# Tying GpSimd's row scatter to TensorE's gate products in an attention and mixture-of-experts kernel

## What is computed

```python
def ffn(x):                                   # 8192 tokens x 256
    scores = softmax(x @ gate_w.T)            # 8 experts
    idx = top_k(scores + gate_b, 2)           # each token goes to 2 of the 8
    cw = sum(one_hot(idx) * scores_at(idx))
    a = swiglu((x @ w1[e] + b1[e]) * (x @ w3[e] + b3[e]))   # every expert e, width 512
    routed = sum over e of cw[:, e] * (a @ w2[e] + b2[e])
    shared = swiglu((x @ sw1 + sb1) * (x @ sw3 + sb3)) @ sw2 + sb2
    return routed + shared
```

## Time and profile before

| | us |
|---|---|
| median of 3 executions | 2370.92 |
| the three | 2356.42, 2370.92, 2376.85 |
| the profiled execution | 2381.0 |
| its span, first to last instruction | 2379.3 |

### The profile page before, as it was taken

The page is one execution under the profiler, slowest core; times in us unless marked ns, Lnnn a source line. Parts: engine busy times, 40 slices in busy tenths (PEclk is TensorE's granted clock), DMA queues, the critical chain, the costliest instruction groups (busy, mean ns, idle before and its releaser), DMA issues. The chain is left out here.

```text
span 2379.3 us, 38346 instructions
## 1 busy us (share of the span) xinstructions
PE 2135.5 (90%) x14197; PEld 1310.5 (55%) x14197; DVE 1558.3 (65%) x2267; ACT 1720.2 (72%) x2176; POOL 687.6 (29%) x694
## 2 busy tenths in 40 slices
PE   5995999999999999999996956789999999999970
PEld 4773333333333333333335855568788888888860
DVE  4663255555555555555556965456788888888878
ACT  4664999999999999999994743223466666666645
POOL 1111000000000000000002525556056666666644
PEclk9997999999999999999998967789999999999995
DMA  5886744555555544444405845656477777777666
GB/s 186 301 301 176 130 90 89 100 99 100 100 97 99 88 72 91 85 87 62 74 10 163 285 146 200 198 182 208 165 218 195 173 169 171 171 171 172 173 171 233
DMA packets 174588, 356.88 MB, mean 150 GB/s; under 512 B 18440, under 2 KB 101000, under 8 KB 167112
## 3 DMA queue, kind: packets, MB, share of 16 engines
q1 hardware_dynamic: 140140, 299.86, 47.2%
q0 software_dynamic: 31952, 46.82, 11.0%
q10 hardware_dynamic: 2316, 7.80, 0.9%
HBM read 210.85 MB, written 143.42 MB: 149 GB/s over the span
## 5 line engine op out<-in xcount | busy, mean ns | idle before, releaser
L1076 ACT ACTIVATE att_prob<-att_scores 128x1024 f32<-128x1024 f32 (+2 forms) x1122 | 997.6, 1035 | 58.6 <-PE att_scores L1022 56.1
L1041 PE MATMUL att_out<-att_prob,att_va 128*32 128x512 f32 (+3 forms) x5000 | 576.7, 542 | 12.9 <-DVE att_prob L1108 12.9
L1022 PE MATMUL att_scores<-att_qs,att_ks 50*128 50x512 f32 (+3 forms) x2560 | 465.9, 430 | 20.7 <-DMA att_qs<-guard 16.7
L1022 PEld LDWEIGHTS att_scores<-att_qs,att_ks 50*128 50x128 f32 x2560 | 211.1, 185 | 492.5 <-ACT att_prob L1076 418.2
L1690 POOL DMA_INDIRECT sums<-moe_y,moe_token x156 | 348.7, 2235 | 235.3 <-ACT moe_y L1941 189.2
L1828 PE MATMUL moe_ps<-moe_xt_hi,moe_w_hi 128*128 128x512 f32 x880 | 352.9, 401 | 11.0 <-ACT moe_h L1914 9.4
L1828 PE MATMUL moe_ps<-moe_xt_lo,moe_w_hi 128*128 128x512 f32 x880 | 348.8, 396 | 5.6 <-issue 5.6
L1828 PE MATMUL moe_ps<-moe_xt_hi,moe_w_lo 128*128 128x512 f32 x880 | 350.3, 398 | 3.6 <-issue 3.6
L970 POOL DMA_DIRECT2D ctx_scr<-att_cout x64 | 55.5, 867 | 983.1 <-DVE att_cout L1158 944.2
L1108 DVE SCALAR_TENSOR_TENSOR att_prob<-att_prob,att_tri 128x512 f32<-128x512 f32 x224 | 144.8, 688 | 268.5 <-ACT att_prob L1076 268.5
L1914 ACT ACTIVATE moe_h<-moe_ps,moe_wb 128x512 f32<-128x512 f32 x220 | 148.4, 676 | 168.9 <-PE moe_ps L1828 100.5
(11 more groups left out here) (232 smaller groups left out, 3216.1 us busy)
## 6 DMA issues: line engine op xcount, KB each, us to landing
qk_parts<-proj_qk SPq DMA_DIRECT2D x64, 512.0 KB
keep_first_weights<-w_experts SPq DMA_DIRECT2D x22, 1412.0 KB
moe_wraw<-w_experts SPq DMA_DIRECT2D x21, 1412.0 KB
att_qs<-qk_parts SPq DMA_DIRECT2D x180, 128.0 KB
att_ks<-qk_parts SPq DMA_DIRECT2D x180, 128.0 KB
rows_in<-att_zeros SPq DMA_DIRECT2D x13, 1548.0 KB, 21.5
moe_moved<-tokens SPq DMA_DIRECT2D x32, 512.0 KB
keep_first_rows<-rows_in SPq DMA_DIRECT2D x20, 516.0 KB
```

The source lines that it names most:

```text
L1022: last = nc.tensor.matmul(pss[e % SBUFS][:, h, at:at + CH - q0], ks[s][rows, half, kt * P:(kt + 1) * P], qs[s][rows, half, c * CH + q0:(c ...
L1041: last = nc.tensor.matmul(pso[k % 2][strip, q0:], va[team % 2][:, kt, strip], probs_of(u)[:, h, at:at + CH - q0], start=(kt == 0), stop=(i ...
L1076: nc.scalar.activation(probs_of(u)[:, half * 2:half * 2 + 2, start:], pss[e % SBUFS][:, :, start:], ACT.Exp, scale=HD ** -0.5)\
```

## The change

Ahead of every scatter GpSimd now also waits for a count of gate products. For scatter q the count is `(q - 8) * 13 * 4 // 128`, rounded down; where it is zero or less there is no wait. It is 1 for q = 11, 12 for q = 38 and 39, 13 for q = 40, and 48 for q = 127, which is the last gate product of step 11. The count is turned into a step and a block, and the wait is on that step's `p1` semaphore. Nothing is removed and nothing else moves: the same 128 scatters, in the same order, from the same buffers.

```diff
+        SCATTERS = 2 * TPC * NCH
+        LEAD = 2 * TPC
+
+        def follow_products(pool, q):
+
+            blocks = (q - LEAD) * (FIRST - 1) * FB // SCATTERS
+            if blocks > 0:
+                c, f = divmod(blocks - 1, FB)
+                pool.wait_ge(p1[c % 2], c // 2 * FB + f + 1)
+
         with nc.Block() as block:
             @block.gpsimd
             def _(pool):
@@
                     for r in range(2):
                         for j in range(TPC):
                             t = c * TPC + j
+                            follow_products(pool, (c * 2 + r) * TPC + j)
                             pool.indirect_dma_start(
                                 out=rows_in, out_offset=bass.IndirectOffsetOnAxis(slot[:, r, t:t + 1], 0),
                                 in_=moved[s][:, r, j, :], in_offset=None).then_inc(scattered[s], 16)
```

## The result

The changed kernel took 2343.76 us (median of 7, 2342.20 to 2348.66) against 2371.42 for the kernel before (7 executions, 2356.42 to 2376.85). The ratio is 0.9885 with a 95% interval of 0.9863 to 0.9908: 27.7 us less, 1.15%. I had forecast 12 us less, with a range that held the time. The direction and the place were right and the size was too small by more than half: two terms of the sum, what the first stall would still cost and what would follow it, were each too small by nearly 8 us. The experiments then showed something larger: the stalls that the change shortens are there in some sessions on the chip and absent in others, for the same kernel, and where they are absent the change is worth nothing. In the traces the recording itself differs between the two kinds of session, so whether the gain exists when nothing is recorded is open.

A forecast was written before the change was run, and what follows sets the result against it. It took TensorE as the bound, with 48.2 us lost in three stalls during scattering. Lost after: 18.3 + 12 + 5.8 = 36.1, a gain of 12.1 from 2370.92, so 2359 us; 8-in-10 range 2332 to 2382.

The forecast's parts named there:

- A: Stall at 1483 to 1517 us, in steps 1 and 2: 27.9 us lost before, 18.3 forecast to remain.
- C: Stall at the end of step 11, 1664 to 1672 us: 5.8 us lost, forecast to stay since no wait holds.
- What bounds the kernel: TensorE mostly busy; the change can give back only three stalls, 48 us, where unbroken scattering holds back three engines.
- The waits cost nothing: 117 waits on GpSimd at 0.05 us each, 6 us, off the chain except at its last scatter.
- After A: Steps 3 to 9: two short stalls of about 6 us, 12 us in place of the 14.5 lost before.
- the leash cures it: Rival: 1 us of rest is enough, no stall after A; gain 29.9, 2341 us; chance 0.26.
- No change that can be measured: Rival: stalls differ without the profiler, perhaps from its own records; gain 0, 2371 us; chance 0.21.
- Slower: Rival: the leash makes stalls regular, steps 3 to 9 lose 8 us each, 2403 us; chance 0.08.
- B: Stall at 1548 to 1563 us, between steps 3 and 6: 14.5 us lost, to be replaced by 12.

The follow-up runs named there:

- e11_lag: The changed kernel with every count 16 gate products lower, in a session with stalls: 2364.10 us, ratio 1.0002.
- e1_lag: The changed kernel with every count 16 gate products lower, in a session without stalls: 2328.43 us, ratio 0.9993.
- e14_loads: The changed kernel with the second double load of moved chunks at step 9 in place of step 13, in a session with stalls: 2344.85 us, ratio 0.9916.
- e13_pad: The kernel before with one small memset on GpSimd ahead of every scatter and no wait on TensorE, in a session with stalls: 2368.73 us.
- e5_lead0: The changed kernel with LEAD = 0 in place of 8, in a session without stalls: 2336.82 us, ratio 1.0031.
- e12_half: The kernel before without the scatters of each token's second expert, 64 in place of 128, in a session with stalls: 2326.67 us, ratio 0.9847.
- before_again: The kernel before, unchanged, run again in a session without stalls: 2329.14 us, ratio 0.9996 to its other executions.
- e9_heavy: The kernel before with a 512 KB DRAM-to-DRAM copy behind each load of a moved chunk, in a session with stalls: 2361.53 us, ratio 0.9978.

## Why the prediction was too small

Two terms of the sum failed: the 18.3 us that A would still cost, because the first wait to hold was read off the matmul records, and the 12 us for two short stalls behind A. By the profiles A gave back 17.4 us and not 9.6, the steps after it 10.2 and not 2.5, and C 2.4 and not 0.

**What bounds the kernel: right for that session, with one error.** The prediction has something hold back three engines; as shown above, only TensorE is seen to be held, and the other two wait for its signals. The three stalls were what the change could give back, and the rest of the kernel stayed as it was: from the turn of step 14 to that of step 53 both profiles take 569.9 us. I put the stalls at 48 us and a lower bound of about 2333 without them; half of the scatters, in session 5, gave 2326.7.

**The waits cost nothing: right.** I took 6 us of GpSimd's time; the gap ahead of a scatter whose wait is met stayed at 0.30 us, and with waits that are met (e11_lag, e1_lag) the ratios are 1.0002 and 0.9993.

**Stall A: the mechanism right, the size 8 us off.** I had GpSimd stop at scatter 38 (1500.2) and TensorE go on 3.1 us later, with 18.3 us lost. It stopped at scatter 36, where count 11 was not yet signalled, at 1493.34; TensorE's gaps ended at once and its signals were level with its records again by 1498.9. 10.5 us were lost. The trace of before could have told most of this: I took a gate product as done when its last matmul is recorded. By the signals count 10, which scatter 33 wants, came only at 1498.21, while scatter 33 stood at 1493.74, 6.5 us ahead of scatter 38. Besides, by the profiles of the sessions with stalls the start of the first one is not fixed (step 2 in two, 3 in e14_loads, 4 in e11_lag), so that no single trace could give this term to better than its own size. I had taken one trace's onset as given. The shift from session to session is luck that the forecast had no term for.

**After A: too small by as much.** I gave the leashed GpSimd two stalls of 6 us in steps 3 to 9, because the stretch ahead of C had the same busy share and stalled. Measured: 1.0, 0.8, 1.8 and 1.0 us in steps 4, 5, 6 and 8, 4.6 in all in place of 12, where the kernel before lost 14.8. Two things were wrong in the term. The busy share is the wrong measure (e13_pad is busy 84% and clean, as said). And I priced a stop at 3 us of scatters plus 3 us of lag; in steps 4 to 6 stops of 1.81, 1.36 and 1.99 us, all behind late signals, stand beside losses of 1.0, 0.8 and 1.8 us in those steps. The rival "the leash cures it" was nearest, 2341 against 2343.8 measured, and that is partly luck: it left 18.3 us in A and nothing else, and the profile has 10.5 in A, 4.6 behind it and 6.5 in C.

**C: the stall stayed, but a wait did hold.** I had count 48 reached at 1664.9, ahead of scatter 127. That is the matmul's record; its signal came at 1670.80 in the trace of before. In the changed kernel the last scatter was held for 1.85 us (the row above). The stall was a little shorter in step 12 (6.5 beyond a clean step, 8.9 before). e14_loads, which splits the last two chunks, had none in its profile; that is one profile of a thing that moves.

**No change that can be measured** had 0.21, and I argued against it that 48 us less would put the profiled execution at 2333, below all that were seen. In four of the six later sessions the kernel before does run at 2329.5, and the change gives nothing. The argument was sound for the session whose trace I had; it did not ask whether the stalls are the kernel's. The rival had the gain in the profile and not in the median. It is in both, but the timed executions carry a recorded span as well, so this does not speak against the rival's cause, the recording.

**Slower** did not come about, though its first half is real: e13_pad and e5_lead0 show what lateness costs (41 us and 7 us). It comes from late rows and not from regular stalls.

**What is settled and what isn't.** Shown: the stalls need dense scatters (e12_half), fewer scatters in a time prevent them (e13_pad), waits that are met do nothing (e11_lag), and dense scatters alone are not sufficient (before_again). Seen in one profile, and not isolated by an experiment: that a stop of 2 us ends a stall that has begun. So of the 28 us I can't say how much comes from the slower mean pace (the count lets 8 scatters through in 11.9 us; measured 12.4) and how much from the stops. The changed kernel itself was not run again in a session with stalls.

Open too: what else it takes. It differs between sessions of one kernel on one numbered chip (7: without stalls in session 3, with them in session 4, nine minutes later). It could be a neighbour's traffic, or the recording itself. That the scatters' writes are slower is not it by what the profiles show: between 1483 and 1517 their packets of 4128 bytes took 122 ns in the mean in before and 121 in before_again.

For the recording there is a sign in the traces. The record of one execution of the kernel before has 24273 semaphore updates where it stalls and 26352 in before_again, with the same number of instructions. Up to 1400 us the two have 16077 each. Between 1400 and 1700 us, where the scatters run, they have 1796 and 4067, so more than half of the records are missing from the first; behind 1700 us they have 6400 and 6208. In this stretch all eight profiles of sessions with stalls lack 23 to 68 of the 234 to 311 signals that TensorE, ScalarE and VectorE give each other there, those of e12_half and e13_pad too, in which nothing stalls. None of the twelve profiles of the other sessions lacks one. So the recording ran short in the same sessions and the same stretch as the stalls. This makes the recording a strong suspect and does not show it: something else may slow both the kernel and its recording. No execution here is known to be unrecorded.

## What to carry to other kernels

If engines that wait for nothing are starved in a profile while one engine issues indirect DMAs back to back, look first whether another session shows it too: here the same kernel lost 40 us in some and nothing in others. Look also whether semaphore updates are missing from the slow stretch of the profile, before the gain is taken for one that unrecorded executions have. Tying the issuer to a count of the starved engine's work is cheap insurance, since waits that are met cost nothing that could be measured. A profile shows when an instruction is recorded, and a wait goes by the signal: in a stall the two were up to 23 us apart, so take from the signal when a wait will hold. The limit of such a tie is the consumer of what is issued: a lead of 8 cost nothing that could be measured, a lead of 0 cost 7 us, and an even spacing by filler 40.

## What the runs showed of the hardware

- TensorE can be held back for some 6 to 30 us while GpSimd issues 128-row scatters at its usual 1.27 us each and the DMA engines are 52% (A) or 28% busy (B, C). In A it ran 47 matmuls in 34 us, and its signals came up to 23 us after the matmuls' records. VectorE and ScalarE starve behind it, and start within 0.2 us of a signal. I had not expected a DMA issuer to do this with the DMA engines partly free.
- It vanishes when 8 scatters take 14 us in place of 11.5, and when GpSimd is busy 54% with scatters, and it is absent altogether in some sessions at 11.5 us. At 12.4 (the changed kernel) and 12.6 us (e9_heavy) some of it was left.
- Semaphore updates are missing from the profiles of just those sessions, up to 56% of them between 1400 and 1700 us.
- 128 scatters of 128 rows in 182 us, beside a DMA share of 0.8, cost TensorE nothing in a session without stalls.
